# Router scores of a mixture-of-experts block: which operand stays in the array, with the start of the kernel reordered around it

## The reference, cut to what matters

```python
xn = _layernorm(x)                              # x: 4 sequences x 1024 tokens x 1024
s  = linear attention of xn                     # phi(q) * cumsum(phi(k) * v), then Wo
# mixture of experts, 8 experts, top 2, capacity 256 each, one shared pair of weights:
logits = xn @ router_w.T                        # 4096 tokens x 8
probs = softmax(logits);  top_p, top_i = top_k(probs, 2)
pos   = running count of each expert's picks    # first choices of all tokens, then second ones
keep  = pos < 256                               # later picks are dropped
h     = gelu(buf @ w1.T + b1) @ w2.T + b2       # buf: kept tokens only
out   = x + s * silu(scatter of h * top_p)
```

## Time and profile before

| | us |
|---|---|
| median of 3 runs (2004.38, 2004.76, 2006.69) | 2004.76 |
| profiled execution, its own time | 2003.46 |
| its span, first to last instruction | 2001.3 |
| TensorE busy | 1971.3 (99%) |
| VectorE busy | 1385.0 (69%) |
| ScalarE busy | 707.6 (35%) |
| GpSimd busy | 511.3 (26%) |

### The profile page before, as it was taken

One profiled execution on the slowest core, in us unless ns is written; L12 is line 12 of the kernel. 1 busy time (PEld: TensorE's weight loads), 2 busy tenths in 40 slices (PEclk: granted clock), 3 DMA queues, 4 the chain that ended last, 5 costly groups with the idle time before them and its releaser, 6 DMA issues.

```text
span 2001.3 us, 27188 instructions
## 1 busy us (share of the span) xinstructions
PE 1971.3 (99%) x9396; PEld 904.9 (45%) x9396; DVE 1385.0 (69%) x2099; ACT 707.6 (35%) x1112; POOL 511.3 (26%) x640
## 2 busy tenths in 40 slices
PE   8999999999999999999999999999999999999996
PEld 2355555555444444444444444444444444444442
DVE  3788788888877777776777797564455565456656
ACT  1442222222754345344335443522212322222322
POOL 0038888888302311321310010110000000000002
PEclk9999999999999999999999999999999999999998
DMA  9546667666899888977877879673333233334535
GB/s 353 215 148 226 215 224 232 233 232 201 295 338 281 260 245 265 276 238 273 263 257 238 292 249 328 203 222 103 102 102 100 93 112 99 116 106 157 184 113 129
DMA packets 182219, 416.26 MB, mean 208 GB/s; under 512 B 18592, under 2 KB 71392, under 8 KB 179680
## 3 DMA queue, kind: packets, MB, share of 16 engines
q1 hardware_dynamic: 138736, 284.26, 42.7%
q0 software_dynamic: 34912, 121.71, 19.9%
q10 hardware_dynamic: 8464, 8.92, 1.4%
HBM read 268.51 MB, written 163.10 MB: 216 GB/s over the span
## 4 chain that ended last, share of the span: by engine, by line
PE 91%; DVE 3%; DMA 2%; issue 1%; ACT 1%; POOL 0%; SPq 0%; ACTq 0%; DVEq 0%; POOLq 0%
PE pair L2132 36%; PE pair L2103 32%; PE pair L1942 18%; PE pair L1892 2%; PE pair L1971 2%; DMA spare<-up_sums 1%; PE pair L1993 1%; DMA arena<-x_t 1%; DMA routing<-kvs_dram 0%; PE pair L1905 0%; DVE arena L1653 0%; DMA arena<-up_sums 0%; PE pair L2072 0%; DVE arena L1313 0%; ACT arena L1033 0%
## 5 line engine op out<-in xcount | busy, mean ns | idle before, releaser
L2132 PE MATMUL pair<-arena 128*128 128x512 f16 x3360 | 730.2, 379 | 1.6 <-DVE arena L1678 0.5
L2103 PE MATMUL pair<-xnT,arena 128*128 128x512 f16 x2400 | 525.4, 379 | 2.0 <-ACT xnT L1040 1.9
L2132 PEld LDWEIGHTS pair<-arena 128*128 128x128 f16 x3360 | 327.8, 98 | 400.7 <-issue 7.7
L1678 DVE SCALAR_TENSOR_TENSOR arena<-pair,arena 128x1024 f32<-128x1024 f32 x234 | 286.1, 1223 | 150.6 <-PE pair L2132 149.7
L1942 PE MATMUL pair<-arena 128*128 128x512 f16 x1728 | 382.6, 379 | 0.8 <-ACT xnT L911 0.8
L1114 ACT ACTIVATE arena<-arena 128x512 f16<-128x512 f32 x280 | 171.9, 628 | 555.6 <-PE pair L2132 500.7
L2103 PEld LDWEIGHTS pair<-xnT,arena 128*128 128x128 f16 x2400 | 234.3, 98 | 286.6 <-ACT xnT L1040 3.7
L1942 PEld LDWEIGHTS pair<-arena 128*128 128x128 f16 x1728 | 168.8, 98 | 192.6 <-ACT xnT L911 1.2
L2103 PE MATMUL pair<-xnT 128*128 128x512 f16 x960 | 213.7, 379 | 0.0
L1653 DVE SCALAR_TENSOR_TENSOR arena<-arena 128x512 f16<-128x512 f32 x280 | 189.6, 689 | 16.5 <-ACT arena L1114 15.8
L835 POOL DMA_DIRECT2D s_dram<-arena x8 | 6.2, 778 | 596.4 <-DVE arena L1678 596.4
(11 more groups left out here) (213 smaller groups left out, 1836.8 us busy)
## 6 DMA issues: line engine op xcount, KB each, us to landing
down_dram<-arena SPq DMA_DIRECT2D x70, 512.0 KB, 6.6
arena<-down_dram SPq DMA_DIRECT2D x70, 512.0 KB, 3.3
up_dram<-arena SPq DMA_DIRECT2D x90, 256.0 KB, 6.1
arena<-up_dram SPq DMA_DIRECT2D x90, 256.0 KB, 2.6
arena<-down_sums SPq DMA_DIRECT2D x40, 512.0 KB, 6.1
arena<-w_up POOLq DMA_DIRECT2D x36, 512.0 KB, 5.3
up_sums<-arena POOLq DMA_DIRECT2D x36, 512.0 KB, 3.7
arena<-up_sums SPq DMA_DIRECT2D x66, 256.0 KB
```

The lines of the kernel that those rows point to most:

```text
L1678: ins = nc.vector.scalar_tensor_tensor(to, src, scale, to, ALU.mult, ALU.add)
L2103: ins = mm(out_to, w[:, a, c * P:(c + 1) * P], x_in_op[:, b, c, :], start=(first and i == 0), stop=(i == 11), skip_group_check=True)
L2132: ins = mm(down_banks(j, t // 2)[:, (t % 2) * BLOCK:(t % 2 + 1) * BLOCK], g_ops[:, A_NAMES.index(DOWN_A[j]), c, a, t * P:(t + 1) * P], dow ...
```

## The change

- Router scores: the 128 tokens of a quarter block (`xt_in[u][:, i, c, :]`, 128 x 128, float32) are now the operand held in the array, and the 9 columns of `rw_f` move. The output is by token at once. The array `x_t` is laid out by quarter blocks for it; each load has the same bytes and a contiguous run per partition, as before. The 9-row copy on ScalarE, the turn by identity and the semaphores between them are gone.
- Start: TensorE no longer waits for `const_ready`. VectorE first fills 1 KB per partition with zeros, and TensorE multiplies them 16 times (128 x 128 held, 512 columns moved, float16). GpSimd makes the column of ones and `ones_f` first. The sums of the router's weights are one matmul, after two quarters of block 0, on a sum over chunks that VectorE makes.
- `WKV_BEHIND` is now none, none, 2, 2, 2, 2, 4, 3; the last piece's low half is made on VectorE after `kept_ready`, ahead of the memset of L1374. The load order on SyncE follows. TensorE's third output waits for 12 pieces before its first half and for all 16 before its second.
- The fill of `meta_dram` writes 128 rows of 128 bytes instead of 2048 of 8 bytes.

```diff
-        xt_in = [part(2 + 4 * u, 4).rearrange("p (c t) -> p c t", c=CH) for u in range(2)]
+        xt_in = [part(2 + 4 * u, 4).rearrange("p (i c t) -> p i c t", i=BLOCK // P, c=CH) for u in range(2)]
...
+        nothing = part(16, 1)[:, 0:BLOCK // 2]
+        rw_chunks = table(N4, "p (e o) -> p e o", e=EXPERTS, o=1)
...
-        WKV_BEHIND = ((), (), (0,), (1, 2), (3, 4), (5, 6, 7, 8), (9, 10, 11), (12, 13, 14, 15))
+        WKV_BEHIND = ((), (), (0, 1), (2, 3), (4, 5), (6, 7), (8, 9, 10, 11), (12, 13, 14))
...
-            load_wkv(0)
-            for b, weights in ((2, (1, 2)), (3, (3, 4)), (4, (5, 6)), (5, (7, 8)), (6, (9, 10, 11)), (7, (12, 13, 14, 15))):
+
+            for b in range(2, TOKEN_BLOCKS):
                 for half in range(2):
                     load_xt(b, half)
-
-                    for q in weights[half::2] if b < TOKEN_BLOCKS - 1 else weights * half:
-                        load_wkv(q)
+                    if b < TOKEN_BLOCKS - 1:
+                        load_wkv(2 * b - 4 + half)
+            for q in range(2 * TOKEN_BLOCKS - 6, 2 * CH):
+                load_wkv(q)
...
+            ch.step(nc.gpsimd.memset(rw_f[:, :, EXPERTS:EXPERTS + 1], 1.0))
+            ch.step(nc.gpsimd.memset(ones_f, 1.0))
...
-            pool.dma_start(meta_dram.rearrange("(t p) c -> p t c", p=P), meta_s[:, :, :]).then_inc(meta_filled, 16)
+            pool.dma_start(meta_dram.rearrange("(p t) c -> p t c", p=P), meta_s[:, :, :]).then_inc(meta_filled, 16)
...
             for b, weights in enumerate(WKV_BEHIND):
-                act.wait_ge(scores_done, b + 1)
-                if b >= 2:
-
-                    act.wait_ge(logits_done, b - 1)
-                nc.scalar.activation(by_expert[b % 2][0:EXPERTS + 1, :], scores(b % 2), ACT.Copy).then_inc(scores_read, 1)
                 if b == TOKEN_BLOCKS - 2:
 
+                    act.wait_ge(scores_done, b + 1)
...
+            high_wkv(2 * CH - 1)
...
+            nc.vector.memset(nothing, 0.0).then_inc(zeros_ready, 1)
...
+            dve.wait_ge(router_loaded, 16)
+            nc.vector.tensor_reduce(rw_chunks[:, :, :], rw_f[:, :, 0:EXPERTS].rearrange("p c e -> p e c"),
+                                    AX.X, ALU.add).then_inc(zeros_ready, 1)
...
-                dve.wait_ge(logits_done, b + 1)
+                dve.wait_ge(scores_done, b + 1)
...
             nc.vector.tensor_copy(kept_h[:, :], kept).then_inc(kept_ready, 1)
+            low_wkv(2 * CH - 1)
             nc.vector.memset(kv_hl[:, :, :], 0.0).then_inc(kvlo_ready, 2)
...
+            def scores(u, i):
+
+                for c in range(CH):
+                    ins = mm(by_token(u)[:, i, :], xt_in[u][:, i, c, :], rw_f[:, c, :], start=(c == 0), stop=(c == CH - 1))
+                return ins
+
+            def half_block(u, loaded):
+                pe.wait_ge(xt_loaded[u], 16 * loaded)
+                scores(u, 0)
+                scores(u, 1).then_inc(xt_half, 1)
+                pe.wait_ge(xt_late[u], 16 * loaded)
+                scores(u, 2)
+
+
+            pe.wait_ge(zeros_ready, 1)
+            zeros = nothing.bitcast(F16)
+            for _ in range(16):
+                mm(out_bank(2), zeros[:, 0:P], zeros, start=True, stop=True)
             pe.wait_ge(router_loaded, 16)
...
+            pe.wait_ge(pool_consts, 1)
             pe.wait_ge(xt_first, 16)
-            scores_by_expert(0, range(CH // 4))
+            scores(0, 0)
             pe.wait_ge(xt_loaded[0], 16)
-            scores_by_expert(0, range(CH // 4, CH // 2)).then_inc(xt_half, 1)
-            second_half(0, 1, range(CH // 2, CH)).then_inc(scores_done, 1)
+            scores(0, 1).then_inc(xt_half, 1)
+            pe.wait_ge(pool_consts, 2)
+
+            pe.wait_ge(zeros_ready, 2)
+            mm(bank[3][:, 0:EXPERTS], ones_f, rw_chunks[:, :, 0], start=True, stop=True).then_inc(sums_w_done, 1)
+            pe.wait_ge(xt_late[0], 16)
+            scores(0, 2)
+            scores(0, 3).then_inc(scores_done, 1)
             with pe.Fori(0, TOKEN_BLOCKS // 2 - 1) as g:
                 for u in (1, 0):
-                    block_scores(u, 2 * g + 2 - u, g + 2 - u)
-                    second_half(u, g + 2 - u, range(CH // 2, CH)).then_inc(scores_done, 1)
-            block_scores(1, TOKEN_BLOCKS - 1, TOKEN_BLOCKS // 2)
-            second_half(1, TOKEN_BLOCKS // 2, range(CH // 2, CH - 2))
+                    pe.wait_ge(logits_read, 2 * g + 2 - u + 1)
+                    half_block(u, g + 2 - u)
+                    scores(u, 3).then_inc(scores_done, 1)
+            pe.wait_ge(logits_read, TOKEN_BLOCKS)
+            half_block(1, TOKEN_BLOCKS // 2)
...
-            scores_by_expert(1, range(CH - 2, CH)).then_inc(scores_done, 1)
-            scores_by_token(1, TOKEN_BLOCKS - 1)
+            scores(1, 3).then_inc(scores_done, 1)
...
-            pe.wait_ge(wkv_ready, 2 * CH)
+            pe.wait_ge(wkv_ready, CH + CH // 2)
             project_chunks(0, 2, range(CH // 2))
             pe.wait_ge(kept_ready, 1)
...
+            pe.wait_ge(wkv_ready, 2 * CH)
             project_chunks(0, 2, range(CH // 2, CH)).then_inc(proj_done, 1)
...
-        "x_t": np.asarray(L0_attn_x).reshape(TOKEN_BLOCKS, BLOCK, CH, P).transpose(0, 3, 2, 1),
+        "x_t": np.asarray(L0_attn_x).reshape(TOKEN_BLOCKS, BLOCK // P, P, CH, P).transpose(0, 4, 1, 3, 2),
```

More of the change, by code:

```diff
@@ L237, in build @@
         top_f = table(4 * N4 + 1500, "p (k t) -> p k t", k=TOPK, t=TILES)
-        by_expert = [xnT_f[:, 12288 + BLOCK * u:12288 + BLOCK * (u + 1)] for u in range(2)]
-        ident_f = xnT_f[:, 13312:13312 + EXPERTS + 1]
-        xt_in = [part(2 + 4 * u, 4).rearrange("p (c t) -> p c t", c=CH) for u in range(2)]
+        xt_in = [part(2 + 4 * u, 4).rearrange("p (i c t) -> p i c t", i=BLOCK // P, c=CH) for u in range(2)]
         EARLY, SOON = TOKEN_BLOCKS - 2, TOKEN_BLOCKS + 1
@@ L293, in out_bank @@
             return bank[i // 2][:, (i % 2) * BLOCK:(i % 2 + 1) * BLOCK]
-        sums_w_done = sem("sums_w_done")
-        const_ready, ident_ready = sem("const_ready"), sem("ident_ready")
+        zeros_ready, sums_w_done = sem("zeros_ready"), sem("sums_w_done")
+        const_ready = sem("const_ready")
         router_loaded, biases_loaded = sem("router_loaded"), sem("biases_loaded")
@@ L305, in build @@
         xt_first, xt_half = sem("xt_first"), sem("xt_half")
-        scores_done, scores_read, logits_done = sem("scores_done"), sem("scores_read"), sem("logits_done")
-        logits_read = sem("logits_read")
+        scores_done, logits_read = sem("scores_done"), sem("logits_read")
         wkv_loaded = [sem(f"wkv_loaded{q}") for q in range(WL)]
@@ L469, in quad_before @@
             return 2 * n + (1 if n % GROUPS == GROUPS - 1 else 2)
-        def scores(u):
-            return bank[2][0:EXPERTS + 1, u * BLOCK:(u + 1) * BLOCK]
         def by_token(u):
@@ L505, in load_xt @@
                     sp.wait_ge(scores_done if half else xt_half, b - 1)
-                c = slice(CH // 2 * half, CH // 2 * (half + 1))
-                sp.dma_start(xt_in[b % 2][:, c, :], x_t[b][:, c, :]).then_inc((xt_late if half else xt_loaded)[b % 2], 16)
+                i = slice(2 * half, 2 * half + 2)
+                sp.dma_start(xt_in[b % 2][:, i], x_t[b][:, i]).then_inc((xt_late if half else xt_loaded)[b % 2], 16)
             def load_wkv(q):
@@ L512, in load_wkv @@
                 sp.dma_start(kv_stage[q], w_kv[q]).then_inc(wkv_loaded[q % WL], 16)
-            sp.dma_start(xt_in[0][:, 0:2, :], x_t[0][:, 0:2, :]).then_inc(xt_first, 16)
-            sp.dma_start(xt_in[0][:, 2:4, :], x_t[0][:, 2:4, :]).then_inc(xt_loaded[0], 16)
+            sp.dma_start(xt_in[0][:, 0], x_t[0][:, 0]).then_inc(xt_first, 16)
+            sp.dma_start(xt_in[0][:, 1], x_t[0][:, 1]).then_inc(xt_loaded[0], 16)
             load_xt(0, 1)
@@ L737, in _ @@
             ch = Chain(pool, pool_consts)
+            ch.step(nc.gpsimd.memset(rw_f[:, :, EXPERTS:EXPERTS + 1], 1.0))
+            ch.step(nc.gpsimd.memset(ones_f, 1.0))
             nc.gpsimd.memset(ones[:, :], 1.0)
-            nc.gpsimd.memset(ones_f, 1.0)
-            nc.gpsimd.memset(rw_f[:, :, EXPERTS:EXPERTS + 1], 1.0)
             nc.gpsimd.memset(zero_c[:, :], 0.0)
@@ L1262, in _ @@
                 nc.vector.memset(scratch[i], 0.0).then_inc(s, n)
+            dve.wait_ge(router_loaded, 16)
+            nc.vector.tensor_reduce(rw_chunks[:, :, :], rw_f[:, :, 0:EXPERTS].rearrange("p c e -> p e c"),
+                                    AX.X, ALU.add).then_inc(zeros_ready, 1)
             dve.wait_ge(const_ready, 1)
             nc.vector.tensor_copy(iota[:, :], iota_i)
-            nc.vector.tensor_copy(ident_f, ident[:, 0:EXPERTS + 1]).then_inc(ident_ready, 1)
             own = Chain(dve, dve_route)
@@ L1881, in _ @@
             mm = nc.tensor.matmul
-            pe.wait_ge(const_ready, 1)
-            pe.wait_ge(router_loaded, 16)
[L1886 to L1914, removed]
+            def scores(u, i):
+                for c in range(CH):
```

(3 more changed lines are left out.)

## The result

| | before | changed |
|---|---|---|
| median, us | 2004.57 (4 runs, 2003.54 to 2006.69) | 2045.02 (4 runs, 2043.33 to 2047.35) |
| profiled execution, its own time / span | 2003.46 / 2001.3 | 2046.16 / 2044.0 |
| mean granted clock of TensorE | 0.997 | 0.970 |

The ratio is 1.020, with a 95% interval of 1.0187 to 1.0213. The change costs 40 us where I forecast a gain of 3.6. It is rival 1 of the prediction: the scores run at the low clock.

A forecast was written before the change was run, and what follows sets the result against it. TensorE's scores were taken as the limit from 28.53 to 74.6 us, with transfers close by. An earlier start, less VectorE's later chain, brings `tables_ready` 3.6 us earlier: 2003.46 to 1999.9 profiled, median forecast 2001.2, range 1997.5 to 2006.5.

The forecast's parts named there:

- rival 1: Router scores on TensorE run at the low clock, 0.224 us a record; slower, 2051 us; chance 0.17.
- The level of the clock: Router scores on TensorE: high level kept, 64 records of 0.1225 us, 7.84 us a block against 7.94 before.
- the zeros: 16 float16 matmuls at TensorE's start: end at 7.3 us; ending at 6.5 or 8.1 changes the time by 0.8 us.
- The record at the high level: TensorE's score record, 128 columns loaded and 9 moved: 0.1225 us from L1905; L1887 at double clock would be 0.112.
- the 7.55 that I had worked out for the transfers: DMA transfers during the scores: 3.15 MB a block takes 7.55 us at 417 GB/s.
- rival 2: Score records cost 0.112 us, transfers set 7.55 us a block; gain 5.6 us, time 1998.4 to 1999.9; chance 0.22.
- VectorE's chain: VectorE's work after block 6 is scored at 62.4 decides: L1357 at 78.35 against 83.11, 4.75 us earlier.
- TensorE's wait for piece 16: TensorE waits for all 16 pieces before the second half of its third output, for about 1.1 us.
- The gain that was meant: `tables_ready`, at 94.29 before, comes 3.6 us earlier, and the execution takes 3.6 us less; chance 0.42.
- The fill: Slots' table filled by 128 runs instead of 2048: the transfers' slump goes and x_t loads land ahead of need.
- The Trainium skill's rule: Short idles between matmul groups move TensorE's clock up and down: mixed levels, 2001 to 2051 us, chance inside rival 1's.

The follow-up runs named there:

- 9, 18 and 36 columns: Columns moved per score matmul: 9 is the changed kernel, 2045.02 us; the changed kernel with the 9 moved twice (18) took 2043.18, four times (36) 2043.16.
- 63 columns: The changed kernel with each score matmul moving the 9 router columns 7 times over, the other 54 results not read: 1997.72 us, ratio 0.9965 to the kernel before.
- burst4: The changed kernel, 9 columns moved, with four float16 matmuls of 512 columns ahead of each group of 8 score matmuls: 2090.21 us.
- 126 columns: The changed kernel with each score matmul moving the 9 router columns 14 times over: 1997.36 us.
- 63 columns, old fill: The kernel with 63 columns, but the slots' table filled by 2048 writes of 8 bytes as in the kernel before: 2044.40 us, ratio 1.0202.

## Why the prediction was wrong

- **The level of the clock** is the step that failed. The prediction priced both levels, took the high one (7.84 us a block) and gave the low one a chance of 0.17; measured are 13.65 us a block, at the low level. Its ground was that the one fall in the trace came after 3.7 us or more without a matmul, and that "what does not raise the clock need not let it fall". The row that spoke against it was there: L1887, 3.58 us without a gap at the low level, and no rise; the prediction cites it and lets it count for little. The runs show that such records neither raise the level nor hold it (9, 18 and 36 columns). The sentence itself is true for 63 columns, which hold without raising. For 9 the trace before had no row.
- **The price of rival 1** was 2051; it came to 2045. (127 lies 43.9 us behind 83.11 and not 43, so its own terms give 2051.9.) The record costs 0.2133 us at the low level, not the 0.224 of L1887: over 464 records that is 5.0 us, most of the difference. The fall came 2.3 us after the zeros, where I took 4. VectorE had caught up by then, as said, but its last block is not the path, as the price had it: it waits 1.26 us more, and the chain runs on TensorE from the last scores (to 116.18) through the first output and the counts, which stand behind it in its program, to L1355 at 123.15.
- **The record at the high level** was mis-sized too. I took 0.1225 from L1905; it is 0.109 with 18 columns (32 in 3.49 us, from 6.30 to 9.79) and 0.106 with 9 (16 from 10.14 to 11.84 in burst4), near the halved L1887 (0.112). The nearest row by kind was the better guide than the nearest by level. With 63 columns a block takes 7.47 us (64 x 54.15 / 464), just under the 7.55 that I had worked out for the transfers, which run at the same 417 GB/s. With 126 columns the scores began 1.07 us later (7.59 against 6.52) and the transposes no later (64.11 against 64.22). Both point to the transfers as the limit, though the profile names no wait for x_t with 63 columns. In this the run followed rival 2.
- **VectorE's chain** was right. With 63 columns ScalarE starts its two high halves at 58.73 and VectorE begins the places at 74.40, 15.7 us later; the prediction had 15.95 (62.4 to 78.35). TensorE's wait for piece 16 was 0.91 us, against 1.1 predicted. What the prediction did not have is the low level that followed this wait and the one before it, 0.94 us; with 126 columns none followed.
- **The gain that was meant**: `tables_ready` at 86.69 with 63 columns (the same row as in the earlier trace rows, VectorE by time) against 94.29 is 7.6 us, and the medians give 7.2. Of the 4.0 us beyond my 3.6, 3.7 are there when block 6 has been scored (58.73 instead of 62.4), and 0.25 come in VectorE's chain. On paper 2.6 of the 3.7 are 7 blocks of 0.37 and 0.8 the zeros, which ended at 6.5. But with 126 columns the zeros ended at 7.6 and block 6 was scored at 58.33, so their early end is not what brought the gain.

```profile
86.69 0.06 DVE L1421 MEMSET routing<- 128x1 f32 x1
```

- **The fill**: the slump went, as said. But the prediction saw in it only earlier transfers. With 63 columns it also kept TensorE free of the wait that costs the level, 47 us.
- The Trainium skill's rule that I set against the change ("TensorE: Matmul & The Clock Gate", A second HAM failure mode) has the clock go up and down at short idles. Here it fell once with no idle before it and stayed down for 109 us, so neither the cause nor the mixture agrees.

## What to carry to other kernels

A stretch of matmuls that load a full held operand and move few columns can run at half the clock although TensorE never idles; read the pace of the nearest such row, and ask of it whether the clock rose under it. Where the moved columns lie under the load anyway, move more of them (here the same 9 seven times) and lift the level first. Then keep long waits out of that stretch: one of 2.8 us lost the level for all the rest of it, one of 0.38 us (126 columns) did not. Only float32 with 128 columns held was tried here.

## What the runs showed of the hardware that I had not expected

- A float32 record with 128 columns held takes 0.106 to 0.110 us at the high level with 9, 18, 36 or 63 columns moved, and 0.112 with 126 (32 from 7.59 to 11.16). At the low level it takes 0.2133 with 9 and 0.215 with 63.
- Raising and holding are not the same: with 63 columns a nearly gapless stream (19.85 us busy of 20) held the level for 54 us, and without the zeros it did not raise it in over 100.
- While 2048 writes of 8 bytes ran on one queue, the rate of all transfers, mostly 1 MB loads of another queue, was 72 GB/s from 10 to 12 us and 176 from 12 to 14 (63 columns, old fill). With 128 writes of 128 bytes it was 426 and 412 (63 columns) and 426 and 410 (the kernel before with that fill).
